# A four-block network on one core: when the shared experts' weights are loaded and split at the end of the second attention

## Chip, cores and metric

One Trainium2 chip, one of its NeuronCores. The metric is the device time of one launch in microseconds (us), start to end on that core. Inputs and outputs are float32, one sequence of 1024 tokens of width 512.

## What is computed

```python
x = _layernorm(x + _L0_attn_ref(x, ...))   # per token: 32 x 32 attention between the heads
x = _layernorm(x + _L0_ffn_ref(x, ...))    # three dense layers with +-1 weights
x = _layernorm(x + _L1_attn_ref(x, ...))   # 32 heads of 16, rotary, window of 128 keys back
x = _layernorm(x + _L1_ffn_ref(x, ...))    # 16 experts (top 2) plus a shared expert of 4 x 128
```

The second attention (`_L1_attn_ref`) and the mixture of experts behind it (`_L1_ffn_ref`) matter here:

```python
scores = einsum('bhqd,bhkd->bhqk', q, k) / sqrt(16)        # masked to the last 128 keys
out = einsum('bhqk,bhkd->bhqd', softmax(scores), v) @ Wo.T
gu_s = x2 @ shared_w_gate_up.T                             # shared expert, float32 accuracy
shared_out = silu(g_s) * u_s @ shared_w_down.T
```

## The kernel before, in words

The tokens lie in eight tiles of 128 (T = 8). Matrix products keep float32 accuracy by splitting each operand into a high part (a copy rounded to the matmul format, made by ScalarE) and a low part (operand minus high part, made by VectorE), and multiplying high x high, high x low, low x high.

**The loop of the second attention.** All engines run the same hand-written order: a loop `for i in range(-1, T)` with eight steps each (TensorE line 644, VectorE line 1272, ScalarE line 1691, GpSimd line 1877). In iteration i, three tiles are in work at once:

- tile r = i + 1: `row_scores(r, s)` (line 571) writes scores, query rows by keys, into two PSUM banks; `row_maxima(r, s)` (line 1201) on VectorE reduces them to row maxima, which `maxima_split`, `turn_maxima` and `maxima_out` turn and which GpSimd's `stack_maxima` (line 1853) puts into the stacked queries by a small DMA;
- tile i: `key_scores` (line 587) computes the scores the other way round, ScalarE takes their exponentials (`weights_out`, line 1642), GpSimd masks them, and `weigh` (line 600) multiplies them with the values at steps 3, 5, 7 and once behind step 7;
- tile d = i - 1: `context_rows` (line 550) turns the weighed values in steps 0 and 1, `context_divided` (line 1174) on VectorE divides them, `turn_context`, `high_dense`/`low_dense` split them, and `output` (line 565) multiplies them with Wo in steps 5 to 7; `add_output` adds the result to X.
- and up to i = 5, tile t = i + 2 is projected to queries, keys and values.

`context_rows`, `turn_maxima` and `turn_context` share one PSUM bank (ring U), so each waits until the reader of the one before is done. `row_scores` share two banks (ring V), `key_scores` two others (ring Q).

**Queries and keys go through DRAM.** For each tile t, SyncE (SP) writes the parts of the keys and of the queries to DRAM (`relay_rows`, line 874; six DMAs a tile, counted by `parts_out`), and GpSimd reads them back as one 1024 KB DMA each (`stack_rows`, line 1843; keys at step 4, queries at step 5 of iteration t - 2), counted by `stack_in`. `row_scores(t, 0)` waits for both (lines 574 and 575). So the last tile, t = 7, is stacked at the end of iteration 5, and iteration 6 begins with `row_scores(7, 0)`.

**The shared expert's weights** come in four pieces e = 0 to 3 of 768 KB (128 x 1536 floats). `load_shared(e)` (line 869, on SP) loads into `wblock[e % 2]`, for e >= 2 once `we_split` says that the low part of piece e - 2 is made. Buffer `wblock[0]` lies on the memory of `parts_q[1]` (lines 161 and 176), from which the last queries are written to DRAM. `shared_high(e)` (ScalarE, line 1650) waits for the load and copies to `W[:, 2e]`; `shared_low(e)` (VectorE, line 1224) waits for the high part, writes `W[:, 2e + 1]` and counts `we_split`. Before the change: SP waits at lines 898 and 899 until the last query parts are written, issues the loads 0 and 1, the gate weights (32 KB) and a table (155.5 KB), then load 2 and load 3, each behind its wait; after them stand the eight stores of the normalised tiles (`xs`). ScalarE makes high parts 0 and 1 in iteration 6 at steps 2 and 5, and high part 2 in iteration 7 at step 2. VectorE makes low parts 0 and 1 behind the last step of iteration 6, and so ahead of `context_divided(U, 6, 0)`, its first work of iteration 7. Parts 2 and 3 follow after the attention.

Of the kernel before, what the change touches and what calls it, by code (L numbers as in the profile page):

```python
# [18 lines left out]
T = 1024 // P  # L19
# [60 lines left out]
def build(nc, x, wq, wk, wv, bias, k0, k1, k2, s0, s1, s2, aq, ak, av, ao, gate, experts, shared,  # L80
          rope_c, factor_c, table_c, out, xs, ys):
    with ExitStack() as ctx:
# [3 lines left out]
        def sem(name):  # L86
            return ctx.enter_context(nc.semaphore(name))
# [185 lines left out]
        parts_out = [sem("qparts_out"), sem("kparts_out")]  # L273
        stack_in = [[sem(f"qstack_in{b}") for b in range(2)], [sem(f"kstack_in{b}") for b in range(2)]]
# [51 lines left out]
        def parts(t, n):  # L326

            return parts_k if n == 1 else parts_q[0 if t < 2 else 1]
# [490 lines left out]
        def _(sp):  # L819
# [49 lines left out]
            def load_shared(e):  # L869
                if e >= 2:  # L870
                    sp.wait_ge(we_split, e - 1)
                sp.dma_start(wblock[e % 2], shared[e]).then_inc(shared_in[e % 2], 16)
# [23 lines left out]
                    sp.wait_ge(stack_in[0][1], 16)  # L896
                    load_raw(3, ao)
            sp.wait_ge(rotated, 2 * T)
            sp.wait_ge(parts_out[0], 48 * T)
            load_shared(0)  # L900
            load_shared(1)
            sp.dma_start(gates.rearrange("p (c e) -> p c e", c=DC), gate.rearrange("(c p) e -> p c e", p=P)).then_inc(gate_in, 16)
# [28 lines left out]
        def _(v):  # L931
# [8 lines left out]
            def tt(o, a, b, op):  # L940
                return nc.vector.tensor_tensor(o, a, b, op)  # L941
# [194 lines left out]
            def rotate(t, n):  # L1136

                name = ("qkv", t, n)
                b = R.take(v, name)[:, :].rearrange("p (h d) -> p h d", d=HD)
                o = rh.rearrange("p (h d) -> p h d", d=HD)  # L1140
                r = rt.rearrange("p (h d) -> p h d", d=HD)
                cos, sin = (rope[:, t, a:a + 1, :].broadcast_to([P, H, HD]) for a in range(2))
                k = HD // 2
                if (t, n) != (0, 1):
                    v.wait_ge(rotated, 2 * t + 1 - n)
                tt(r, b, cos, ALU.mult).then_inc(turned_halves, 1)
                tt(o[:, :, 0:k], b[:, :, k:HD], sin[:, :, 0:k], ALU.mult).then_inc(turned_halves, 1)
                if n == 1 and 1 <= t <= 3:
                    R.drained(v, ("qkv", t - 1, 2))
                tt(o[:, :, k:HD], b[:, :, 0:k], sin[:, :, k:HD], ALU.mult).then_inc(R.free, 1)  # L1150
# [11 lines left out]
            def parts_low(t, n):  # L1162
                b = U.take(v, ("turned", t, n))
                v.wait_ge(parts_high, 2 * t + 2 - n)
                tt(parts(t, n)[:, 1, :], b[:, :], parts(t, n)[:, 0, :].bitcast(F32), ALU.subtract).then_inc(U.free, 1)
# [8 lines left out]
            def context_divided(ring, i, a):  # L1174
                b = ring.take(v, ("context2", i, a))[:, :].rearrange("p (h r) -> p h r", r=32)
                r = hsum[:, a, :].rearrange("p (h r) -> p h r", r=1)
                own(nc.vector.reciprocal(r, b[:, :, HD:HD + 1]))
                turned = co.rearrange("p (c m e d) -> p m c e d", c=4, m=4, e=2)
                for m in range(2):
                    g = slice(8 * m, 8 * m + 8)  # L1180
                    ins = tt(turned[:, 2 * a + m], b[:, g, 0:HD].rearrange("p (c e) d -> p c e d", e=2),
                             r[:, g, :].broadcast_to([P, 8, HD]).rearrange("p (c e) d -> p c e d", e=2), ALU.mult)
                    if m == 0:
                        ins.then_inc(dve, 1)
                        steps[0] += 1
                ins.then_inc(ring.free, 1)
# [14 lines left out]
            def row_maxima(i, s):  # L1201
                n = P if i == 0 else 2 * P
                _, m0 = window(i)
                for f in (2 * s, 2 * s + 1):
                    b = V.take(v, ("rowscores", i, f))[:, :].rearrange("p (a k) -> p a k", a=2)[:, :, 0:n]
                    h = 4 * s + f % 2
                    for m in range(2):
                        ins = nc.vector.tensor_tensor_reduce(masked[:, 2 * (f % 2) + m, 0:n], b[:, m, :], maskb[:, m0:m0 + n], 1.0, -BIG,  # L1208
                                                             ALU.add, ALU.max, hmax[:, h + 2 * m:h + 2 * m + 1])
                    ins.then_inc(V.free, 1)  # L1210
# [13 lines left out]
            def shared_low(e):  # L1224

                v.wait_ge(we_high, e + 1)
                tt(W[:, 2 * e + 1, 0:WCOLS], wblock[e % 2], W[:, 2 * e, 0:WCOLS].bitcast(F32), ALU.subtract).then_inc(we_split, 1)
# [44 lines left out]
            for i in range(-1, T):  # L1272
                t, r, d = i + 2, i + 1, i - 1
                for s in range(8):
                    if r < T:
                        row_maxima(r, s)
                    if s < 2 and d >= 0:
                        context_divided(U, d, s)
                    if s == 1 and 2 <= t < T:
                        rotate(t, 1)  # L1280
                        rope_sum(t, 1)
                    if s == 1 and i >= 0:
                        maxima_out(i, 1)
                    if s == 2 and 2 <= t < T:
                        parts_low(t, 1)
                        rotate(t, 0)
                        rope_sum(t, 0)
                    if s == 3 and r < T:
                        maxima_split(r, 0)
                    if (i, s) == (-1, 3):  # L1290
                        low_dense(("x2", 2), xa[2][1], xa[2][0])
                    if s == 3 and 2 <= t < T:
                        parts_low(t, 0)
                    if s == 4 and d >= 0:
                        low_dense(("co", d), ca[1], ca[0])
                    if i == -1 and s in (2, 4, 5, 6):
                        ffn_out(1, (2, 4, 5, 6).index(s))
                    if s == 5 and r < T:
                        maxima_out(r, 0)
                    if (i, s) == (-1, 6):  # L1300
                        rates(slice(G, T), 4)
                    if s == 6 and 2 <= t < T - 1:
                        low_dense(("x2", t + 1), xa[t + 1][1], xa[t + 1][0])
                    if s == 7 and r < T:
                        maxima_split(r, 1)
                    if s == 7 and d >= 0:
                        add_output(R, d)
                if i == T - 2:
                    shared_low(0)
                    shared_low(1)  # L1310
            context_divided(V, T - 1, 0)
            context_divided(V, T - 1, 1)
            rates(slice(0, T - 1), 5)
# [186 lines left out]
        def _(s):  # L1500
# [20 lines left out]
            def normalise(t):  # L1521
                act(X[:, t, :], X[:, t, :], ACT.Identity, scale=rstd[:, t:t + 1], bias=offset[:, t:t + 1]).then_inc(x_ready, 1)
# [168 lines left out]
            for i in range(-1, T):  # L1691
                t, d = i + 2, i - 1
                for step in range(8):
                    if step == 0 and d >= 0:
                        context_out(d, 1)
                    if i >= 0 and (step % 2 == 0 or i >= 1):
                        weights_out(i, 2 * (step // 2), step % 2)
                    if step == 2 and 2 <= t < T:
                        parts_out_high(t, 1)
                    if step == 3 and 2 <= t < T:  # L1700
                        values_out(t, ("qkv", t, 0))
                        parts_out_high(t, 0)
                    if step == 4 and d >= 0:
                        high_dense(("co", d), coT[:, 0])
                    if (i, step) == (-1, 0):
                        values_out(1, ("qkv", 1, 0))
                    if (i, step) == (-1, 3):
                        high_dense(("x2", 2), x2T[2][:, 0])
                    if (i, step) == (-1, 6):
                        roots(slice(G, T), 4)  # L1710
                        s.wait_ge(offset_ready, 5)
                        for t4 in range(G, T):
                            normalise(t4)
                    if (i, step) == (0, 6):
                        high_part(15, 3, raw_c[3], wc_in[3])
                    if step == 6 and i >= 0:
                        context_out(i, 0)
                    if step == 6 and 2 <= t < T - 1:
                        high_dense(("x2", t + 1), x2T[t + 1][:, 0])
                    if i == T - 2 and step in (2, 5):  # L1720
                        shared_high(step // 3)
                    if i == T - 1 and step == 2:
                        shared_high(2)
            context_out(T - 1, 1)
            def high_x3(t):
# [241 lines left out]
```

## Time and profile before

| | us |
|---|---|
| median of 3 runs | 696.48 (696.41 to 696.8) |
| the profiled execution, device time | 697.87 |
| its span in the trace | 696.1 |
| PE, DVE, ACT, POOL busy in the span | 600.8, 399.0, 270.8, 222.0 |
| SP's DMA queue (q1) | 56.70 MB |
| POOL's DMA queue (q0) | 31.61 MB |

Times in rows are counted from the start of the span. PE is TensorE's matmuls, PEld its weight loads, DVE VectorE, ACT ScalarE, POOL GpSimd, SPq the DMAs that SyncE issues. A PE row in brackets gives the idle time ahead of it and what ended it; "issue" there means that the profile names no engine as the releaser, which includes a wait on a DMA. Iteration 6 of the loop begins at the end of the 422.87 row and iteration 7 at about 452.4.

### The profile page before, as it was taken

Reading aid. Unit: us, or ns where it says so; the run is one execution under the profiler, and the core shown is the slowest. Engines: PE = TensorE matmul, PEld = TensorE weight load, DVE = VectorE, ACT = ScalarE, POOL = GpSimd, SP = SyncE. Lnnn points to the kernel's source line nnn. Section 1 sums busy time; section 2 is a strip of 40 time slices with the busy share of each in tenths; the row PEclk is TensorE's granted clock in tenths of the full one; section 3 lists DMA queues with packets and bytes.
Section 4 is the critical chain, followed back from the end, with each engine's and each line's share of the span. In section 5 each row is a group of like instructions: output and inputs, shape, how many; then the busy total and the mean of one; then the engine's idle time right before and its main releaser. Section 6 shows DMA issues by size and latency. Waiting matters only on the chain.

```text
span 696.1 us, 13473 instructions
## 1 busy us (share of the span) xinstructions
PE 600.8 (86%) x5125; PEld 473.8 (68%) x5125; DVE 399.0 (57%) x1142; ACT 270.8 (39%) x433; POOL 222.0 (32%) x313
## 2 busy tenths in 40 slices
PE   2998999768889977989999996968799999999993
PEld 1987986656767655766767765645377888787662
DVE  3414644797676766878778686632576243323246
ACT  5065118357754234344353443545410122222213
POOL 5001434353500015444363453551002133231360
PEclk9999999989999987899999997767999999999997
DMA  8200110362224616142361444021104499999363
GB/s 301 69 0 20 46 46 18 83 174 85 61 84 155 192 55 214 47 169 99 117 213 50 169 142 175 4 93 57 65 6 174 185 332 400 402 418 366 123 182 121
DMA packets 45680, 99.41 MB, mean 143 GB/s; under 512 B 11760, under 2 KB 18032, under 8 KB 43440
## 3 DMA queue, kind: packets, MB, share of 16 engines
q1 hardware_dynamic: 27280, 56.70, 22.3%
q0 software_dynamic: 12720, 31.61, 14.1%
q10 hardware_dynamic: 5616, 10.23, 4.0%
q8 instruction: 42, 0.69, 0.4%
q14 instruction: 22, 0.18, 0.1%
HBM read 67.96 MB, written 25.95 MB: 135 GB/s over the span
## 4 chain that ended last, share of the span: by engine, by line
PE 53%; DVE 16%; ACT 11%; DMA 9%; issue 8%; POOL 1%; another core or an unknown queue 1%; SPq 1%; ACTq 0%; DVEq 0%
PE bank L343 13%; PE bank L524 10%; PE bank L379 9%; DMA slots_out<-FP 7%; ACT FP L1504 5%; DVE FP L941 5%; PE bank L610 4%; PE bank L582 3%; PE bank L595 3%; DVE kraw L1208 2%; DVE XR L941 2%; PE bank L402 2%; PE bank L555 2%; PE bank L390 2%; ACT XR L1504 1%
## 5 line engine op out<-in xcount | busy, mean ns | idle before, releaser
L1504 ACT ACTIVATE FP<-bank 128x512 f32<-128x512 f32 (+1 forms) x244 | 138.6, 611 | 292.6 <-PE bank L595 104.9
L1208 DVE CUSTOM_DVE_ANT_0 kraw<-bank,maskb 128x256 bf16<-128x256 f32 (+1 forms) x256 | 88.4, 400 | 37.0 <-PE bank L582 37.0
L524 PE MATMUL bank<-W,XR 128*128 128x512 f32 x348 | 98.0, 423 | 1.6 <-DVE XR L941 1.5
L343 PE MATMUL bank<-FP 128*128 128x128 f32 x558 | 88.6, 312 | 1.7 <-ACT FP L1504 1.6
L379 PE MATMUL bank<-W,XR 128*128 128x512 f32 x288 | 77.4, 419 | 5.2 <-DVE W L941 5.2
L524 PEld LDWEIGHTS bank<-W,XR 128*128 128x128 f32 x348 | 65.5, 199 | 16.1 <-DVE XR L941 2.0
L1865 POOL TENSOR_SCALAR_AFFINE_SELECT FP<-FP 128x512 f32<-128x512 f32 x64 | 41.4, 670 | 100.3 <-ACT FP L1504 100.3
L379 PEld LDWEIGHTS bank<-W,XR 128*128 128x128 f32 x288 | 64.2, 271 | 11.7 <-DVE W L941 5.6
L1899 POOL DMA_INDIRECT FP<-slots_in,index x31 | 29.8, 960 | 124.3 <-PE bank L726 64.7
L343 PEld LDWEIGHTS bank<-FP 128*128 128x128 f32 x558 | 65.5, 192 | 3.9 <-issue 2.2
L941 DVE TENSOR_TENSOR FP<-FP,bank 128x128 f32<-128x128 f32 (+1 forms) x39 | 14.4, 369 | 70.9 <-ACT FP L1504 47.7
L343 PE MATMUL bank<-RP,W 128*128 128x512 f32 x192 | 45.7, 394 | 3.5 <-DVE FP L941 3.5
L1868 POOL TENSOR_SCALAR_AFFINE_SELECT FP<-FP 128x512 f32<-128x512 f32 x56 | 37.9, 700 | 21.9 <-ACT FP L1504 21.6
L343 PEld LDWEIGHTS bank<-RP,W 128*128 128x128 f32 x192 | 35.7, 188 | 11.9 <-issue 1.8
L1825 POOL DMA_DIRECT2D RPF<-FP x64 | 31.6, 501 | 34.8 <-PE bank L415 23.9
L941 DVE TENSOR_TENSOR XR<-bank,XR 128x512 fp32r<-128x512 f32 x27 | 21.5, 809 | 31.3 <-ACT XR L1504 31.2
L1435 DVE COPY FP<-bank 128x512 f32<-128x512 f32 x31 | 21.4, 691 | 30.1 <-PE bank L726 30.1
L610 PE MATMUL bank<-FP 128*17 128x128 f32 x960 | 36.5, 300 | 2.0 <-ACT FP L1504 1.8
L582 PE MATMUL bank<-RP,QS 64*128 64x256 f32 x160 | 23.2, 370 | 13.2 <-DVE hmax L1208 9.0
L610 PEld LDWEIGHTS bank<-FP 128*17 128x17 f32 x960 | 25.8, 105 | 12.0 <-issue 6.0
L582 PEld LDWEIGHTS bank<-RP,QS 64*128 64x128 f32 x160 | 14.4, 217 | 24.4 <-issue 14.8
L595 PE MATMUL bank<-QS,RP 64*128 64x128 f32 x320 | 26.0, 284 | 3.6 <-ACT FP L1504 2.5
(179 smaller groups left out, 979.3 us busy)
## 6 DMA issues: line engine op xcount, KB each, us to landing
FP<-in_experts_dram SPq DMA_DIRECT2D x31, 768.0 KB
slots_out<-QS SPq DMA_DIRECT2D x48, 256.0 KB, 2.9
RP<-slots_out POOLq DMA_DIRECT2D x8, 1024.0 KB, 5.4
slots_out<-FP ACTq DMA_DIRECT2D x31, 256.0 KB
QS<-slots_out POOLq DMA_DIRECT2D x5, 1024.0 KB, 7.1
XR<-slots_out POOLq DMA_DIRECT2D x3, 1024.0 KB, 7.1
FP<-in_shared_dram SPq DMA_DIRECT2D x4, 768.0 KB, 6.1
RPF<-FP POOLq DMA_DIRECT2D x64, 34.0 KB, 2.0
```

The lines of the kernel that those rows point to most:

```text
L343: mm = nc.tensor.matmul(bank, lhs, rhs, start=(n == 0), stop=(n == len(terms) - 1))
L379: mm = nc.tensor.matmul(b[:, :], *terms[m], start=(m == 0), stop=(m == 3 * DC - 1))
L524: mm = nc.tensor.matmul(b[:, :], *terms[n], start=(n == 0), stop=(n == len(terms) - 1))
L582: mm = nc.tensor.matmul(both[a][:, m, :], qS[i % 3][half(a, KS), pr, :], kS[half(a, KS), slots, pr, :], start=True, stop=True)
L595: mm = nc.tensor.matmul(both[a][:, m * P:(m + 1) * P], kS[half(a, KS), (i - w) % 4, pr, :], qS[i % 3][half(a, KS), pr, :], start=True, sto ...
L610: mm = nc.tensor.matmul(weighing[32 * q:32 * q + HD + 1, (h // 4 % 4) * P:(h // 4 % 4 + 1) * P], vaug[:, (i - w) % 4, head(h), :], PT[hg % ...
L941: return nc.vector.tensor_tensor(o, a, b, op)
L1208: ins = nc.vector.tensor_tensor_reduce(masked[:, 2 * (f % 2) + m, 0:n], b[:, m, :], maskb[:, m0:m0 + n], 1.0, -BIG, ALU.add, ALU.max, hmax ...
L1504: return nc.scalar.activation(o, i, func, **kw)
L1825: nc.gpsimd.dma_start(vdiag[k % 3][32 * g:32 * g + 32, 272 * g:272 * g + 272].rearrange("p (s d) -> p s d", s=CH), vT[32 * g:32 * g + 32, ...
L1865: ins = nc.gpsimd.affine_select(out=pt, in_=pt, compare_op=ALU.is_ge, fill=0.0, base=0, pattern=[[0, 4], [1, P]], channel_multiplier=-1)
L1868: ins = nc.gpsimd.affine_select(out=pt, in_=pt, compare_op=ALU.is_ge, fill=0.0, base=-1, pattern=[[0, 4], [-1, P]], channel_multiplier=1)
```

## The change

On SP, the loads 0 and 1 (with all that stands behind them in SP's order) wait for the landing of the last stacked queries in place of the last writes of the query parts. On VectorE, low parts 0 and 1 move from behind iteration 6 to steps 2 and 5 of iteration 7. On ScalarE, high part 2 moves from step 2 to step 7 of iteration 7.

```diff
@@ SyncE
             sp.wait_ge(rotated, 2 * T)
-            sp.wait_ge(parts_out[0], 48 * T)
+            sp.wait_ge(stack_in[0][(T - 1) % 2], 16 * (T // 2))
             load_shared(0)
             load_shared(1)
@@ VectorE, in the loop over s
                     if s == 3 and 2 <= t < T:
                         parts_low(t, 0)
+                    if i == T - 1 and s in (2, 5):
+                        shared_low(s // 3)
                     if s == 4 and d >= 0:
                         low_dense(("co", d), ca[1], ca[0])
...
                     if s == 7 and d >= 0:
                         add_output(R, d)
-                if i == T - 2:
-                    shared_low(0)
-                    shared_low(1)
             context_divided(V, T - 1, 0)
@@ ScalarE, in the loop over step
                     if i == T - 2 and step in (2, 5):
                         shared_high(step // 3)
-                    if i == T - 1 and step == 2:
+                    if i == T - 1 and step == 7:
                         shared_high(2)
```

## Rows read from the trace of the kernel before

**Rows 1.** The page: busy tenths and granted TensorE clock in 40 slices.
```profile
PE   2998999768889977989999996968799999999993
...
PEclk9999999989999987899999997767999999999997
```

**Rows 2.** The chain that ended last, 395 to 520 us: start, us, what.
```profile
422.87 3.27 issue
...
453.08 3.74 DVE W L941 x2
...
463.62 1.82 DMA QS<-QS
```

**Rows 3.** The timeline of POOL: stacked queries of tile 6, keys and queries of tile 7.
```profile
387.68 0.58 POOL L1851 DMA_DIRECT2D XR<-slots_out  x1
...
413.59 0.59 POOL L1851 DMA_DIRECT2D RP<-slots_out  x1
...
415.71 0.58 POOL L1851 DMA_DIRECT2D QS<-slots_out  x1
```

**Rows 4.** DMA issues from 378 to 405 us: count, KB, median us to landing.
```profile
RP<-slots_out POOLq DMA_DIRECT2D x1, 1024.0 KB, 5.2
XR<-slots_out POOLq DMA_DIRECT2D x1, 1024.0 KB, 7.1
```

**Rows 5.** DMA issues from 405 to 432 us.
```profile
FP<-in_shared_dram SPq DMA_DIRECT2D x2, 768.0 KB, 9.7
RP<-slots_out POOLq DMA_DIRECT2D x1, 1024.0 KB, 8.0
QS<-slots_out POOLq DMA_DIRECT2D x1, 1024.0 KB, 10.3
```

**Rows 6.** DMA issues from 350 to 378 us, queries of tile 5.
```profile
QS<-slots_out POOLq DMA_DIRECT2D x1, 1024.0 KB, 7.6
```

**Rows 7.** The timeline of SP: the first two shared loads.
```profile
414.23 1.00 SPq L872 DMA_DIRECT2D FP<-in_shared_dram  x2
```

**Rows 8.** DMA issues from 454 to 456 us: the third shared load, alone.
```profile
FP<-in_shared_dram SPq DMA_DIRECT2D x1, 768.0 KB, 4.0
```

**Rows 9.** The timeline of PE, steps of iterations 5 to 7.
```profile
410.76 0.50 PE L582 MATMUL bank<-RP,XR 64*128 64x256 f32 x4
...
420.60 2.27 PE L610 MATMUL bank<-FP 128*17 128x128 f32 x64
...
438.42 0.79 PE L582 MATMUL bank<-RP,QS 64*128 64x256 f32 x4
...
450.24 2.17 PE L610 MATMUL bank<-FP 128*17 128x128 f32 x64
...
454.32 0.66 PE L595 MATMUL bank<-QS,RP 64*128 64x128 f32 x8 [0.74 <-ACT FP L1504]
457.66 1.09 PE L555 MATMUL bank<-ident,FP 128*128 128x128 f32 x4 [2.67 <-DVE FP L941]
...
465.48 1.12 PE L595 MATMUL bank<-QS,RP 64*128 64x128 f32 x8
...
478.52 1.07 PE L610 MATMUL bank<-FP 128*17 128x128 f32 x32
```

**Rows 10.** Stretches: length, busy PE, PEld, DVE, ACT, POOL, granted clock, DMA share, GB/s.
```profile
426.10:438.40 12.30, 10.40 (x89) 8.26 (x89) 8.53 (x41) 5.61 (x9) 5.80 (x10) 0.50 0.02 2
...
439.60:442.70 3.10, 1.98 (x22) 1.55 (x21) 2.29 (x12) 2.50 (x5) 1.48 (x3) 1.00 0.02 5
443.20:446.10 2.90, 2.90 (x37) 1.58 (x35) 0.58 (x5) 1.04 (x1) 0.47 (x1) 0.50 0.00 0
```

**Rows 11.** The timeline of DVE in iteration 7: the low part of context 6.
```profile
468.38 0.69 DVE L941 TENSOR_TENSOR XR<-bank,XR 128x512 fp32r<-128x512 f32 x1 [7.98 <-ACT XR L1504]
```

**Rows 12.** The timeline of ACT: high parts 0 and 2, exponentials of the last step.
```profile
435.27 1.49 ACT L1504 ACTIVATE W<-FP 128x1536 fp32r<-128x1536 f32 x1
...
462.19 1.49 ACT L1504 ACTIVATE W<-FP 128x1536 fp32r<-128x1536 f32 x1
...
475.88 1.09 ACT L1504 ACTIVATE FP<-bank 128x512 f32<-128x512 f32 x2 [0.32 <-PE bank L595]
```

## The prediction, made before the change was run

> **What bounds the kernel now.** I read the page first, for how busy TensorE is and at which clock, then the chain of waits around the change, then the timelines of the engines there and the landing times of the DMAs. On the page PE is busy nearly all the time up to the loop's end, but in the slices around 60 to 70% of the span, where the loop ends, the granted clock sinks to seven and six tenths [rows 1]. The loop is one chain through all engines, so what is lost on the chain there is lost in the total. The chain names two things in iterations 6 and 7: 3.27 us ahead of the first row scores of tile 7, for which no engine is the releaser, and 3.74 us of two VectorE operations that write W, which are low parts 0 and 1 [rows 2].
>
> The first is the landing of the stacked queries of tile 7. POOL issued that DMA at 415.71 [rows 3] and it took 10.3 us [rows 5], which makes 426.0; PE goes on at 422.87 + 3.27 = 426.14. The queries of tile 6, issued at 387.68, took 7.1 us. What differs is the company: SP issued two shared loads at 414.23 [rows 7], one after the keys (413.59) and before the queries (415.71), and the keys took 8.0 us against 5.2 a tile earlier [rows 4, 5].
>
> The second stands ahead of `context_divided(6, 0)` on VectorE. PE had finished the key scores of step 1 at 454.32 + 0.66 = 454.98 and could turn the next context rows only at 457.66, an idle time of 2.67 us that VectorE ended [rows 9].
>
> After the 3.27 us of idling the granted clock is 0.50, the 1.2 GHz level, through 426.1 to 438.4 [rows 10]. So the stall costs more than its own length.
>
> **Term 1, the wait for the last queries.** With the loads behind the landing, the DMAs of tile 7 have the company that those of tile 6 had: the interval between keys and queries is 2.1 us in both. With 7.1 us they land at 422.8, when the weighing before them ends (420.60 + 2.27 = 422.87 [rows 9]); with the 7.6 us of tile 5 [rows 6] at 423.3, and 0.4 us stay. The gain is 2.8 to 3.27; I take 3.2, since tile 6 has the same interval and is nearest.
>
> **Term 2, the low parts.** Both go from VectorE ahead of iteration 7. PE's context rows of step 1 then wait for the key scores alone and come at 454.98: 2.7 us. That is the lower end; the whole 3.74 would be the upper end, but PE's own key scores cover the difference. At the new places they cost nothing: between step 2 and the low part of context 6 VectorE idles 7.98 us [rows 11], and one low part takes half of 3.74, 1.9 us. The second, at step 5, stands between that low part (468.38 + 0.69) and the addition of the output, which needs the product of step 7 and so comes no earlier than the exponentials of that step at 475.88 [rows 12]; several us are free there. If VectorE were late at either place, at most 1.9 us would be lost.
>
> **Term 3, the loads on SP.** Four DMAs move together (load 0, load 1, gate, table), from 414.23 to about 423. Who waits: ScalarE's high part 0 at step 2 of iteration 6. Before, that copy ran at 435.27 [rows 12], 9.1 us after the first row scores; at the 2.4 GHz level I expect it some 7 us after them, at 430. A load alone landed in 4.0 us [rows 8], two together beside the stacked keys and queries in 9.7 in the median [rows 5]. Two together and alone lie between, nearer the first: 5 to 6 us, at 429. So nothing is lost; with 9.7 us ScalarE would be held for some 2.7 us, and with it the exponentials queued behind it. The gate and the table are wanted after the loop, and the stores of X stand behind load 3, which needs low part 1 at step 5 of iteration 7, while the tiles that they store are normalised behind the loop's end. Nothing.
>
> **Term 4, high part 2.** Out of step 2 (1.49 us [rows 12]) it gains nothing: what step 4 waits for there is the small DMA of the maxima, not the exponentials behind the copy (463.62 + 1.82 = 465.44 against key scores at 465.48 [rows 2, 9]). At step 7 the exponentials end at 475.88 + 1.09 = 476.97, and the context copy waits for the last weighing, which ends at 478.52 + 1.07 = 479.59: 2.6 us for a copy of 1.49. Free, if load 2 has landed. It is now issued behind low part 0 at step 2, some 14 us before; 4.0 us is what it needs.
>
> **Term 5, a collision that the change makes.** Load 2 is now issued as low part 0 ends, which is just when POOL sends the maxima of tile 7, and step 4 waits for that DMA. Alone it took 1.82 us. What a shared load adds to a small transfer no row shows cleanly; the keys lost 8.0 - 5.2 = 2.8 us to two loads, and below nothing a collision cannot go. Load 2 starts only shortly before, so 0 to 2.8; I take 0.5, nearer the lower end, because 16 KB have little to share. The Trainium skill ("DMA: Bandwidth & Descriptors", Queues, rings and completion order) says that each DMA engine alternates between the queues at packet granularity; by that the small DMA would wait for a packet at a time, and its cost would be near the lower end too, while the large stacked queries should lose much, as they do.
>
> **Term 6, the clock.** Steps 0 to 3 of iteration 6 took 438.42 - 426.14 = 12.3 us at 1.2 GHz. At 2.4 GHz VectorE's 8.53 us of work in that stretch [rows 10] and four handoffs to PE would set the time, some 9.5 us; that is worth 2.8 (0 to 3.8). Steps 4 to 7 of iteration 6 took 450.24 + 2.17 - 438.42 = 14.0 us with the clock at half for part of them, those of iteration 5, with the clock high, 420.60 + 2.27 - 410.76 = 12.1: 1.9 us. Iteration 7 took 479.59 - 465.48 = 14.1 for the same steps, again 2.0. All of it together would be 6.7 us. But the clock does not fall after long stalls alone: it was high from 439.6 to 442.7 with PE 1.98 of 3.10 us busy, so idle for 1.1 us in all, and then it was 0.50 at 443.2 [rows 10]. Steps 1 to 3 of iteration 6 hold no projection and no weighing until step 3, and the start of iteration 7 even less. I expect it to fall there, later than before and for a shorter time. So I take 2.0 us of the 4.7 in iteration 6 and 1.0 in iteration 7 (its first four steps, which now run partly at 2.4 GHz). Ends: 0 and 6.7.
>
> **The sum.** 3.2 + 2.7 + 0 + 0 - 0.5 + 3.0 = 8.4 us. What follows the loop is a chain that starts from its end, so it comes that much sooner. On the profiled execution that is 697.87 - 8.4 = 689.5 us (span 687.7). The median of the runs stands 1.39 us below the profiled execution; from it, 696.48 - 8.4 = 688.1 us.
>
> **The rivals.**
> *The clock holds through iteration 6.* With the stall gone there is no long idle time left, and the 4.7 us come back whole: 3.2 + 2.7 - 0.5 + 4.7 + 1.0 = 11.1, to 685.4. For it: through the iterations before the clock stayed high, at nines [rows 1]. Against it: those steps had projections, and the fall at 443. By the Trainium skill ("TensorE: Matmul & The Clock Gate", Part 1) the array goes to the low clock after idling; taken alone that would make this case the forecast. The same page (A second HAM failure mode: psum-queue depth-cycling) tells of short idles between groups that make the clock oscillate, and the row at 439.6 sides with that.
> *Only the two stalls come back.* The clock falls as early and for as long as before, or a new gap takes its place: 2.8 + 2.7 - 0.5 = 5.0, to 691.5.
> *The change does not do what it says to the queries:* they land late because of their own queue and the DRAM, and 1.5 us at most come back there; with term 2 and no clock, 4 us, to 692.5. Against it is that keys and queries of tile 7 are both slower than their neighbours, and only that once.
> *Slower.* The later loads hold ScalarE at high part 0 in iteration 6, with the exponentials, masks and weighing queued behind. It needs the first load to land by 430; each us later is a us lost. To be slower than before it must eat 5 us and more, which is a landing after 12 us and over. The two loads took 9.7 us in the median [rows 5] with the 2 MB of stacking beside them, which are now gone from there. A landing after 14 us would give 698.
>
> **How the numbers follow.** A partial return of the clock, 0.55: 688.1, by its own terms 686.5 to 690.5. The clock holds, 0.2: 685.4. Only the stalls, 0.15: 691.5. The queries not relieved, 0.05: 692.5. Slower, 0.03; and 0.02 that gains and losses cancel. Two in ten lie outside when the range takes in most of the holding clock and of the bare stalls: 685.0 to 691.3. About 0.2% (1.4 us) is what a measurement of this kernel can tell from no change; faster by more than that 0.95, within it 0.02, slower 0.03.
>
> **What would show it.** In the changed trace: the stacked queries of tile 7 take 7 to 7.6 us, and PE's gap ahead of the first row scores of tile 7 is under 0.8 us; the two loads land within 6 us of an issue at about 423 and ScalarE's copy at step 2 has no idle ahead of it that a DMA ends; context rows at step 1 of iteration 7 follow the key scores within 0.5 us; the maxima's DMA takes 2 to 2.5 us; high part 2 ends before the last weighing. The clock should be 1.00 past 426 and fall once before 433. A gap that stays before iteration 6, ScalarE held at step 2, or a clock at 0.50 from 426 on would make the prediction wrong.

## The result and the profile after

The changed kernel took 691.56 us (median of 15 runs, 687.67 to 695.46) against 697.09 us for the kernel before on the same chips (15 runs, 693.04 to 700.12): a ratio of 0.9922, 95% interval 0.99 to 0.9944. So it is faster, by 5.4 us (3.9 to 7.0). The forecast was 688.1, 8.4 us faster, with a range of 685.0 to 691.3; the measured median lies 0.3 us above that range. Both kernels spread by 7 to 8 us from one execution to the next, far more than the three runs shown ahead of the prediction did, and that spread is part of the story. Here and below a ratio is taken against executions of the kernel before on the same chip and leaves out those more than 1.5% above the fastest of their kernel, so it is not always the quotient of two medians.

| | before | after |
|---|---|---|
| profiled execution, device time | 697.87 | 694.21 |
| its span | 696.1 | 692.2 |
| PE, DVE, ACT, POOL busy | 600.8, 399.0, 270.8, 222.0 | 598.7, 398.4, 271.1, 221.7 |

Both programs have 13473 instructions; the changed one's span is 3.9 us shorter. 2.1 us of that are PE's own busy time, because the same matmuls take longer at the low clock: 32 of the weighing take 1.91 us at 1.2 GHz and 1.07 us at 2.4. The rest is waiting. The page's clock line of the changed kernel, to be held against [rows 1], has nine and eight for seven and seven at the start of the loop's end; six and seven behind them stayed:

```profile
PEclk9999999999999987899999999867999999999997
```

Ahead of iteration 6 the stall is gone. First the DMA issues from 400 to 430 us of the changed kernel (count, KB, median us to landing; compare [rows 5]), then SP's timeline:

```profile
FP<-in_shared_dram SPq DMA_DIRECT2D x2, 768.0 KB, 4.9
RP<-slots_out POOLq DMA_DIRECT2D x1, 1024.0 KB, 6.0
QS<-slots_out POOLq DMA_DIRECT2D x1, 1024.0 KB, 6.3
```
```profile
422.84 1.14 SPq L872 DMA_DIRECT2D FP<-in_shared_dram  x2
...
453.35 10.29 SPq L872 DMA_DIRECT2D FP<-in_shared_dram  x2
```

The second row of SP puts loads 2 and 3 together: they were issued at 453.35 and 463.31. The queries land in 6.3 us in place of 10.3 (in the other traces with this wait in 6.7 to 7.9), and the loads issued behind them in 4.9. PE's timeline shows what became of the two gaps, and a new one (compare [rows 9]):

```profile
422.56 1.07 PE L610 MATMUL bank<-FP 128*17 128x128 f32 x32 [0.16 <-POOL FP L1867]
423.56 0.50 PE L582 MATMUL bank<-RP,QS 64*128 64x256 f32 x4
...
446.87 0.66 PE L595 MATMUL bank<-QS,RP 64*128 64x128 f32 x8
...
448.86 0.66 PE L595 MATMUL bank<-QS,RP 64*128 64x128 f32 x8 [0.73 <-ACT FP L1503]
449.45 0.65 PE L555 MATMUL bank<-ident,FP 128*128 128x128 f32 x4
...
458.03 1.12 PE L595 MATMUL bank<-QS,RP 64*128 64x128 f32 x8 [1.98 <-DMA QS<-QS]
...
474.26 1.07 PE L610 MATMUL bank<-FP 128*17 128x128 f32 x32
```

Row scores of tile 7 start as the weighing ends (423.56, no brackets, so no idle time). The context rows of step 1 follow the key scores at once (449.45). But ahead of step 4 of iteration 7, at 458.03, PE now idles 1.98 us for the small DMA of the maxima. The stretches of the changed kernel (columns as in [rows 10]) show the clock:

```profile
426.10:429.30 3.20, 1.88 (x25) 1.46 (x23) 2.60 (x14) 1.08 (x2) 1.57 (x3) 1.00 0.95 344
429.80:436.20 6.40, 5.25 (x58) 4.38 (x59) 4.71 (x23) 3.84 (x6) 3.51 (x6) 0.50 0.03 3
436.60:453.00 16.40, 12.80 (x179) 9.43 (x178) 11.01 (x39) 9.74 (x17) 8.70 (x15) 1.00 0.02 3
453.80:473.60 19.80, 17.45 (x149) 11.84 (x149) 3.92 (x5) 7.79 (x13) 8.71 (x14) 0.50 0.25 82
```

In iteration 6 it is at 1.2 GHz for one stretch of at least 6.4 us. In iteration 7 it is at 1.2 GHz for at least 19.8 us, nearly to the loop's end, though PE was busy for 17.45 of them. The two spans, cut at the same four events, in us:

| stretch | before | after | gain | forecast |
|---|---|---|---|---|
| up to the end of iteration 5 (last weighing, first row scores) | 422.87 | 423.56 | -0.7 | 0 |
| to the first key scores of iteration 7 | 29.47 | 23.31 | 6.2 | 5.2 |
| to the key scores of its step 4 | 13.14 | 11.16 | 2.0 | 3.2 |
| to the end of its last weighing | 14.11 | 17.30 | -3.2 | 0 |
| to the end of the span | 216.5 | 216.9 | -0.3 | 0 |

So in this pair of executions the gain came in iteration 6, more of it than forecast, and a part was given back in iteration 7. The first row is a warning: up to there every kernel of this document issues the same work, and still it took 419.3 to 427.3 us in the 14 traces. Single executions are therefore compared below stretch by stretch, not by their total.

### The profile page after: what moved, and what is told of

Same layout as the page of the kernel before. It is cut to its first block, busy times and chain, and to the rows that moved or that the text cites. A ratio compares the mean times of both kernels' runs of the same rounds, so it can differ in the third digit from the quotient of the medians.

```text
span 692.2 us, 13473 instructions
## 1 busy us (share of the span) xinstructions
PE 598.7 (86%) x5125; PEld 472.3 (68%) x5125; DVE 398.4 (58%) x1142; ACT 271.1 (39%) x433; POOL 221.7 (32%) x313
## 4 chain that ended last, share of the span: by engine, by line
PE 52%; DVE 17%; ACT 11%; DMA 8%; issue 7%; POOL 1%; another core or an unknown queue 1%; SPq 1%; ACTq 0%; DVEq 0%
PE bank L343 13%; PE bank L524 11%; PE bank L379 9%; DMA slots_out<-FP 5%; ACT FP L1503 5%; DVE FP L941 5%; PE bank L610 4%; PE bank L595 3%; PE bank L582 3%; DVE kraw L1208 2%; DVE XR L941 2%; PE bank L390 1%; DVE st L968 1%; ACT XR L1503 1%; ACT W L1503 1%
## 5 line engine op out<-in xcount | busy, mean ns | idle before, releaser
L524 PE MATMUL bank<-W,XR 128*128 128x512 f32 x348 | 100.0, 430 | 1.6 <-DVE XR L941 1.5
L379 PE MATMUL bank<-W,XR 128*128 128x512 f32 x288 | 77.6, 420 | 5.2 <-DVE W L941 5.2
L595 PEld LDWEIGHTS bank<-QS,RP 64*128 64x128 f32 x320 | 23.7, 205 | 7.9 <-DMA QS<-QS 3.5
```

The lines of the kernel that those rows point to most:

```text
L379: mm = nc.tensor.matmul(b[:, :], *terms[m], start=(m == 0), stop=(m == 3 * DC - 1))
L524: mm = nc.tensor.matmul(b[:, :], *terms[n], start=(n == 0), stop=(n == len(terms) - 1))
L595: mm = nc.tensor.matmul(both[a][:, m * P:(m + 1) * P], kS[half(a, KS), (i - w) % 4, pr, :], qS[i % 3][half(a, KS), pr, :], start=True, sto ...
```

## The experiments

**What was asked.** Theory A: the two stalls are separate; the change takes both away, and loses something in iteration 7 where load 2 meets the maxima's DMA, where low part 0 slows POOL's mask, and through the clock. Rivals: the moved low parts bring the gain, or are what costs.

**One part of the change at a time.** The wait alone is SyncE's line of the diff on the kernel before. The low parts alone is the changed kernel with that line put back.

```diff
 e1_wait_only, on the kernel before
-            sp.wait_ge(parts_out[0], 48 * T)
+            sp.wait_ge(stack_in[0][(T - 1) % 2], 16 * (T // 2))
 e2_low_only, on the changed kernel
-            sp.wait_ge(stack_in[0][(T - 1) % 2], 16 * (T // 2))
+            sp.wait_ge(parts_out[0], 48 * T)
```

> Only SyncE's wait is changed; low parts 0 and 1 and high part 2 stay where they were before. Theory A (the two stalls are separate, and iteration 7 of the changed kernel gives part back through a DMA collision and the clock): the stall of 3.3 us ahead of iteration 6 and a shorter stretch at 1.2 GHz come back, 4 to 6 us in all at the start of iteration 7, and iteration 7 is as before, 27.2 us: 4 to 6 us below before (ratio 0.991 to 0.994). The gap of 2.7 us at the context rows of step 1 is still there. Theory B (moving the low parts is what brings the gain): ratio 0.996 or more.

> Only the low parts and high part 2 are moved; SyncE loads at the old place. Theory A: the stall of 3.3 us stays with the low clock behind it; context rows of step 1 in iteration 7 come 2.7 us sooner, the maxima's DMA takes 3 us or more in place of 1.8 beside load 2, and the mask of step 2 is slowed by 0.5; 0 to 2 us below before (ratio 0.997 to 1.0). Theory B: the moved low parts bring most of the 5.4 us: ratio 0.994 or less.

Measured: the wait alone 692.47 us, ratio 0.9937 (0.9903 to 0.997), the low parts alone 696.21, ratio 0.9985 (0.9955 to 1.0015), by which it can't be told from no change. In us that is 4.4 (2.1 to 6.8) and 1.0 (-1.0 to 3.1). That they add up to just the 5.4 of the whole change is in part luck, with intervals that wide. Theory B needed a ratio of 0.994 or less from the low parts alone; the interval excludes it. Theory A stands. PE's timelines show each stall by itself, first with the wait alone (iteration 7's context rows), then with the low parts alone (iteration 6's first row scores, and step 4 of iteration 7):

```profile
450.75 0.63 PE L555 MATMUL bank<-ident,FP 128*128 128x128 f32 x4 [2.67 <-DVE FP L941]
```
```profile
430.66 0.79 PE L582 MATMUL bank<-RP,QS 64*128 64x256 f32 x4 [3.36 <-issue]
...
466.20 1.12 PE L595 MATMUL bank<-QS,RP 64*128 64x128 f32 x8 [1.69 <-DMA QS<-QS]
```

The new gap ahead of step 4 comes with the moved low parts, not with the wait.

**The collision, and the mask.** Load 2 is held until the maxima have landed; in the second kernel low part 0 is held instead, and load 2 with it.

```diff
 e3_load_held, on the changed kernel (SyncE)
+            sp.wait_ge(max_in[1], 32 * T)
             load_shared(2)
 e4_low_held, on the changed kernel (VectorE)
                     if i == T - 1 and s in (2, 5):
+                        if s == 2:
+                            v.wait_ge(max_in[1], 32 * T)
                         shared_low(s // 3)
```

> The changed kernel with SyncE waiting for the landing of tile 7's second maxima before load 2, so that the two DMAs do not meet; low part 0 still runs beside the mask of step 2. Theory A: the maxima's DMA goes back to about 1.8 us from its second issue; 1.3 us less at step 4 of iteration 7, up to 2 us faster than the changed kernel (ratio to before about 0.990). Rival, the DMA is slow because VectorE's low part keeps POOL from writing its descriptors, not because of load 2: it stays at 3.1 us and the time at 0.992.

> The changed kernel with VectorE waiting for the landing of tile 7's second maxima before low part 0, which holds load 2 as well. Both theories of the slow DMA expect 1.8 us here; theory A besides expects the two masks of step 2 to take 1.22 us in place of 1.72, so step 4 of iteration 7 comes 1.8 us sooner after the iteration's start than in the changed kernel (9.4 in place of 11.2 us). What the clock makes of it in steps 4 to 7 is open: 1 to 3 us below the changed kernel, ratio to before 0.988 to 0.991.

Measured: 689.47 us, ratio 0.9889 (0.9845 to 0.9933), and 690.61, ratio 0.9924 (0.9888 to 0.996). The second ratio missed the 0.988 to 0.991 that was expected, though its interval covers it. The times alone do not tell these two from the changed kernel, the intervals overlap. The traces do. POOL's timeline at step 2 of iteration 7, the mask and then the maxima's DMAs, in the changed kernel, with load 2 held, and with low part 0 held:

```profile
452.69 1.72 POOL L1864 TENSOR_SCALAR_AFFINE_SELECT FP<-FP 128x512 f32<-128x512 f32 x2 [1.27 <-ACT FP L1503]
454.36 1.12 POOL L1856 DMA_DIRECT2D QS<-QS  x2
```
```profile
456.49 1.72 POOL L1865 TENSOR_SCALAR_AFFINE_SELECT FP<-FP 128x512 f32<-128x512 f32 x2 [1.28 <-ACT FP L1504]
458.16 1.12 POOL L1857 DMA_DIRECT2D QS<-QS  x2
```
```profile
455.09 1.23 POOL L1866 TENSOR_SCALAR_AFFINE_SELECT FP<-FP 128x512 f32<-128x512 f32 x2 [1.28 <-ACT FP L1505]
456.26 1.12 POOL L1858 DMA_DIRECT2D QS<-QS  x2
```

The pair of masks takes 1.72 us beside low part 0 and 1.23 without it. The maxima's DMA (two of 8 KB, the median of both) took 3.1 us to its landing in the changed kernel and 1.8 in both others. In the first of these low part 0 still stood where it was, so it is load 2 that slows the DMA, not VectorE's work. Step 4 came 11.16, 9.96 and 9.47 us behind the iteration's first key scores: 1.20 us for the collision and 0.49 for the mask. The Trainium skill ("SBUF — State Buffer", Who interferes with whom) says that a VectorE operation with two SBUF inputs and a GpSimd operation that reads SBUF exclude each other. The low part and the mask are such operations, and the trace agrees in direction, with 0.5 us. The trace of the kernel before showed it too: a pair of masks that ran while both low parts did (453.08 to 456.82) took 3.56 us, against 1.22 or 1.23 for every other pair from 412 us on.

```profile
453.76 3.56 POOL L1865 TENSOR_SCALAR_AFFINE_SELECT FP<-FP 128x512 f32<-128x512 f32 x2 [2.47 <-ACT FP L1504]
457.27 1.22 POOL L1868 TENSOR_SCALAR_AFFINE_SELECT FP<-FP 128x512 f32<-128x512 f32 x2
```

That spoke against the new place of low part 0 and is not in the prediction.

**The clock.** On the kernel with low part 0 held, TensorE gets matmuls of 512 columns whose results nobody reads, in its idle time. One kernel has them in iteration 7, one in 6 and 7, one in 6.

```diff
 e5_busy_7, on e4_low_held (TensorE; a helper and its call in the loop)
+            def keep_busy(n):
+                m = len(R.number)
+                pe.wait_ge(R.free, m - 1)
+                for _ in range(n):
+                    nc.tensor.matmul(R.banks[m % 2][:, :], W[:, 6, 0:P], W[:, 7, 0:D], start=True, stop=True)
...
+                    if i == T - 1 and s < 5:
+                        keep_busy((4, 4, 5, 0, 3)[s])
 e6_busy_67, besides
+                    if i == T - 2 and s < 5:
+                        keep_busy((2, 4, 4, 0, 2)[s])
 e7_busy_6: the call for i == T - 2 alone
```

> The kernel that holds low part 0 behind the maxima, and 16 more matmuls of 512 columns on TensorE in steps 0, 1, 2 and 4 of iteration 7, whose results nobody reads (into a bank that is free there). They fill idle time. Theory C (what is left in iteration 7 is the granted clock): the clock stays at 2.4 GHz through it, steps 4 to 7 take 11.5 to 12.5 us in place of 13.4 to 17.3, and iteration 7 some 21 us in place of 23.2: 2 us below the kernel without them. Rival (the chain through the other engines binds there): no change, or slower by up to 1 us for the matmuls that stand in the way.

> As the run before, with 12 more such matmuls in steps 0, 1, 2 and 4 of iteration 6. Theory C: the clock stays at 2.4 GHz there too and iteration 6 takes 21.5 to 22.5 us in place of 23.3 to 24.1; 3 to 4 us below the kernel without any, ratio to before about 0.985. Rival: no change.

> The filling matmuls in iteration 6 alone. Theory C: 1 to 2 us below the kernel without any, from iteration 6, and iteration 7 as without them, 23 to 24 us with the clock falling once.

Measured: 685.68 us, ratio 0.9861 (0.9816 to 0.9905); 682.85, ratio 0.9834 (0.9782 to 0.9886); 688.16, ratio 0.9898 (0.9848 to 0.9947), with iteration 6 in 22.51 us and iteration 7 in 24.08, with the clock falling once, as expected. The first two came out lower than expected. The stretches of iterations 6 and 7 of the kernel with both:

```profile
419.30:441.70 22.40, 19.92 (x266) 14.84 (x262) 17.82 (x81) 13.04 (x22) 11.91 (x20) 1.00 0.24 82
441.80:463.30 21.50, 19.02 (x237) 13.85 (x237) 9.01 (x18) 11.57 (x20) 12.53 (x18) 1.00 0.24 76
```

The clock is 1.00 throughout. Steps 4 to 7 of iteration 7 took 11.97 us, against 13.74 without the extra matmuls and 17.30 in the changed kernel's trace; iteration 6 took 22.47 against 24.09, iteration 7 21.55 against 23.21. So the two iterations are 3.3 us shorter than in the trace of the kernel without extra matmuls, and in these traces the clock is what differs: giving TensorE more work made the kernel faster. By the ratios (0.9924 and 0.9834, on different chips) it is some 6 us; where the rest of that comes from, the traces do not show. The kernel with both is about 12 us faster than before and beats the changed kernel.

**The changed kernel again.**

> The changed kernel once more, on the chip of the runs beside it. Theory C: the 17.3 us that steps 4 to 7 of iteration 7 took in its first trace were a matter of when the clock rose, since nothing waited on another engine for long there; another execution shows 13.4 to 17.3, and step 4 again 11.2 us behind the iteration's start with the maxima's DMA at 3 us. Rival (the change itself lengthens steps 4 to 7, by high part 2 or low part 1): 17 us again, with the clock back at the same step or earlier.

Measured: 690.17 us, ratio 0.9917 (0.9881 to 0.9953). In this execution step 4 came 11.15 us behind the iteration's start, as before, with the DMA at 3.1 us; but steps 4 to 7 took 13.91 us in place of 17.30. Its stretches in iteration 7:

```profile
449.20:462.20 13.00, 9.84 (x96) 7.09 (x96) 3.40 (x3) 4.59 (x9) 7.36 (x10) 0.50 0.30 82
462.70:472.70 10.00, 7.26 (x100) 5.03 (x98) 3.59 (x12) 7.12 (x11) 2.44 (x4) 1.00 0.10 40
```

The clock fell 5 us into the iteration here and 6.6 in the first trace, and stayed down for at least 13 us here and 19.8 there. Behind the key scores of step 4 PE waited no longer than 0.3 us at a time in either. The same program, the same waits: 3.4 us between two executions from the clock. The rival, that high part 2 or low part 1 in their new places lengthen these steps, falls: both were there in both traces.

**The old order with the clock held up.** Extra matmuls in the kernel before (12 at the end of iteration 5 into the stall, 12 in iteration 6 and 20 in 7), and in the changed kernel as it is (as e6, without the held low part). Then two runs on one chip, the best kernel and the last one once more; those two kernels are the same as e6_busy_67 and e10_changed_busy.

```diff
 e9_before_busy, on the kernel before, with the helper
+                    if i == T - 1 and s < 5:
+                        keep_busy((4, 8, 5, 0, 3)[s])
+                    if i == T - 2 and s < 5:
+                        keep_busy((2, 4, 4, 0, 2)[s])
...
                 if i >= 0:
                     weigh(i, 3)
+                if i == T - 3:
+                    keep_busy(12)
```

> The kernel before, with matmuls that nobody reads in TensorE's idle time: 12 at the end of iteration 5 (into the stall), 12 in iteration 6, 20 in iteration 7. It keeps both stalls and takes the clock out of them. If the low clock was a good part of what the stalls cost: the clock stays at 2.4 GHz, row scores of tile 7 still wait for the queries until 10 us behind their issue, iteration 6 takes 22.5 us in place of 26.2, iteration 7 some 24 in place of 27.2; 5 to 7 us below before (ratio about 0.99), as much as the change itself brought. If the stalls' own length was all: no change.

> The changed kernel as it is, with the filling matmuls in iterations 6 and 7. With the clock held in both, it stands against the run before (the old order) by the two stalls alone, less the collision and the slowed mask: 3.3 + 2.7 - 1.8 = 4.2 us faster than it; and against the filled kernel with low part 0 held by the collision and the mask alone, 1.8 us slower. Step 4 of iteration 7 stands 11.2 us behind its start, and iteration 7 takes 23.2 us.

> The kernel with low part 0 held behind the maxima and the filling matmuls in iterations 6 and 7, again, now on one chip with the next run. If the collision of load 2 with the maxima's DMA explains why the filling brought nothing to the changed kernel: faster than the next run by 3 to 6 us, iteration 7 in 21.5 to 22.5 us. If that was the other chip: both alike.

> The changed kernel with the filling matmuls and the collision left in, again. Collision theory: the maxima's DMA takes 3.1 to 3.8 us, TensorE idles over 3 us ahead of step 4 of iteration 7 with nothing to fill it, the clock falls there, and iteration 7 takes 24 to 26 us; ratio to before about 0.991. Rival (the other chip): as the run before, ratio 0.984.

Measured: 695.67 us, ratio 0.9991 (0.9959 to 1.0022); 690.39, ratio 0.9926 (0.9895 to 0.9957); 684.15, ratio 0.9823 (0.9793 to 0.9854); 690.84, ratio 0.9929 (0.9896 to 0.9962). The first two missed what was expected: the extra matmuls brought neither kernel anything that the intervals show. They were to hold the clock and did not. In e9 it fell at 437.7 and again at 464.9, and the iterations took 26.1 and 27.8 us where 22.5 and 24 were expected; in e10 iteration 7 took 25.7 us, not 23.2. So this pair does not price the stalls without the clock, and that stays open. Part of where it got lost is seen in PE's timeline, step 4 of iteration 7 of e12 (its traced execution was the slowest of its twelve, 695.11 us):

```profile
461.08 1.12 PE L595 MATMUL bank<-QS,RP 64*128 64x128 f32 x8 [4.42 <-DMA QS<-QS]
```

With load 2 left beside the maxima, PE idles 4.42 us there (4.37 in e10) with no extra matmul in it, and the clock falls during that wait (in e10 right behind it). With low part 0 held, in e11, the clock stays at 1.00 and iteration 7 takes 21.55 us, as it had on the other chip, against 27.78 in e12. On one chip, the medians of the two are 7 us apart.

That difference is not the collision alone. In iteration 6, where the two programs are the same, the maxima's DMA took 1.7 us in e11 and 2.4 in e12, PE waited 0.39 and 1.47 us for it at step 4, the clock then fell in e12 and not in e11, and iteration 6 took 22.20 and 25.85. The DMA traffic from 430.5 to 434.2 us, in 40 slices, shows what is beside it, first in e11, then in e12:

```profile
GB/s 0 0 0 0 0 0 0 0 0 35 37 22 0 0 0 36 42 17 0 0 0 0 0 0 0 0 177 0 0 0 0 0 0 0 0 0 0 0 0 0
q8 instruction: 1, 0.02, 1.6%
```
```profile
GB/s 0 0 0 0 0 0 0 0 0 0 0 0 0 0 189 25 46 11 0 0 12 36 46 0 0 0 0 0 0 0 0 0 0 0 0 0 0 0 0 0
q8 instruction: 1, 0.02, 1.7%
```

The high number is one packet of 16 KB on the queue that the page calls "instruction", so a piece of program text. In e11 it comes at 432.9, when both DMAs of the maxima have landed (431.93 and 432.50); in e12 it comes at 431.8, as they are under way (430.73 to 434.11). All 14 traces agree. In their iterations 6 and 7 they hold 84 small DMAs of maxima. 51 had neither such a packet nor a shared load beside them and took 1.73 to 1.86 us. 23 had such a packet and no load: where it came in the last 0.3 us it did nothing (three cases), the other 20 took 2.04 to 3.09 us. The remaining ten had load 2 beside them: 2.93 to 3.23 us without the packet, and in e10 and e12, which had both, 4.32 and 4.37 for the later one of the pair. So of PE's wait of 4.4 us there some 1.3 go with the packet and 1.2 with load 2, and e11 against e12 does not isolate the collision; e3 and e4, with no packet there, do. In the kernels without extra matmuls no packet meets these DMAs early enough to slow them; the extra matmuls make the program longer, and the packets come at other moments. No run moved such a packet on purpose, so that it is the cause is inferred, from how closely the two go together.

## Why the prediction was right and wrong

- **Term 1, the wait for the queries: right.** They landed in 6.3 us, a little faster than the 7.1 taken (7.0 in the second trace), PE's gap went from 3.27 us to none, and the wait alone is worth 4.4 us with what it gives back of the clock.
- **Term 2, the low parts: right as to the stall, incomplete as to the new place.** The gap of 2.67 us went, and the context rows of step 1 came 2.58 us behind the first key scores, against 5.32 before and 2.64 forecast. "At the new places they cost nothing" failed: low part 0 runs beside POOL's mask of step 2, on the path to the maxima, and costs 0.49 us. I had looked only at who waits on VectorE, not at who works beside it, although the mask of 3.56 us stood in the trace of before.
- **Term 3, the loads: right.** Two loads in 4.9 us, ScalarE's copy right behind its exponentials at step 2.
- **Term 4, high part 2: right.** It ran at 470.68 behind the exponentials of step 7 and ended before the last weighing.
- **Term 5, the collision: right mechanism, mis-sized.** Taken at 0.5 in a bound of 0 to 2.8; e3 measures 1.20. The landing was expected within 2 to 2.5 us and took 3.1. The reason given for the low value, that 16 KB have little to share, did not hold, nor did the packet-by-packet reasoning beside it: at the pace of load 2 (768 KB in some 4.3 us) 16 KB would be an estimated 0.1 us. What else delays the small DMA no run shows.
- **Term 6, the clock: the step that failed, with term 5 and the mask beside it.** For iteration 6 it was forecast that the clock would fall later and for a shorter time, and it did (from 429.6 for some 7 us); the stretch gained 6.2 us against 5.2. The estimate of 9.5 us for its steps 0 to 3 at 2.4 GHz is met by the kernel with extra matmuls in both iterations, 9.52 us. For iteration 7 a gain of 1.0 was taken, for its first four steps, and they gave it: 2.0 us in all there are the stall's 2.7 less 1.2 and 0.5, and 1.0 more. What was put at nothing, without a reason, is the rest of the iteration: steps 4 to 7 took 17.30 us against 14.11 in the trace of before, with the clock low for nearly all of them. In the second trace they took 13.91, so executions lie on both sides. Of the 3.0 us between forecast and measurement, 0.7 are the collision beyond the 0.5 taken and 0.5 the mask. The remaining 1.8 us are the clock's by difference only, and the interval of the measured gain is nearly as wide (3.9 to 7.0). The bound "0 and 6.7" had no loss in it, though nothing in the trace excluded one.

Of the rivals, *the clock holds* did not happen, in line with the gaps of the row at 439.6. *Only the two stalls come back*, at 691.5, is nearest in time, but not in mechanism: in iteration 6 the clock did come back, and its gain was spent in iteration 7. *Slower* is excluded by the time, *queries not relieved* by the landing times. The forecast's other weakness was its base: 696.48 was the median of three runs within 0.4 us, and 15 runs spread over 7 us around 697.09. From its own base the measured ratio gives 691.0 us, inside the range; that the median fell outside is owed to the base, that the gain was 5.4 and not 8.4 us is not.

## What to carry over

When a bulk load is moved off one critical transfer, list the small transfers of its new place; a shared load cost the next small DMA 1.2 us, and holding it behind that DMA's landing cost nothing that its six executions show. VectorE work moved into idle time of VectorE is free only if GpSimd's work beside it is off the path. Where an iteration is limited by handoffs between engines, TensorE's own idle time can be worth filling with matmuls that nobody reads: 28 of them took the ratio from 0.9924 to 0.9834 (e4 to e6), but they brought nothing to the kernels that still had a wait of 2 to 4 us between them. Added instructions also move the moments at which program text is fetched, so look in the trace at what a fetch now stands beside.

## What was not expected of the hardware

The same program differed by some 8 us between executions, and two traces of it differ by 3.4 us in one iteration's last four steps by the stretch at 1.2 GHz (13.91 and 17.30 us). PE was busy 17.45 of 19.80 us at 1.2 GHz and was not granted 2.4 GHz in all that time, where it was granted after a shorter and less busy stretch (9.84 of 13.00 us) in the other execution. And a small DMA that takes 1.7 to 1.9 us alone took 2.0 to 3.1 us when one 16 KB packet of instructions fell into it, in 20 of 20 cases in these traces.
